# Edge blocks rounded up to 128 records, message stage in 52 table-driven runs

## What is computed

```
# x: (1250, 512); src, dst: (40000,), dst sorted
W   = (softplus(f_ij @ Wf1 + bf1) - log 2) @ Wf2 + bf2   # filter of each edge, 6*128 wide
W   = W * rcut_ij[:, None]                               # (in the model part, per edge)
sj, vj = xs[idx_j], xv[idx_j]                            # gathered by source node, 4*128
s2, v2, w1, t = products of sj, vj with the unit direction u of the edge
x_ij = concat(s2 * W[...], v2 * W[...], w1 * W[...], t * W[...])
agg  = segment_sum(x_ij, idx_i, num_segments=n)          # summed by destination node
```

## Time and profile before

| | us |
|---|---|
| median of three runs | 1356.35 |
| lowest, highest | 1356.25, 1357.49 |
| span of the profiled execution | 1356.8 |
| PE busy | 1237.2 (91%) |
| DVE busy | 1136.8 (84%) |
| POOL busy | 894.8 (66%) |
| ACT busy | 837.5 (62%) |

### The profile page before, as it was taken

One profiled execution on the slowest core, in us unless ns is written; L12 is line 12 of the kernel. 1 busy time (PEld: TensorE's weight loads), 2 busy tenths in 40 slices (PEclk: granted clock), 3 DMA queues, 4 the chain that ended last, 5 costly groups with the idle time before them and its releaser, 6 DMA issues.

```text
span 1356.8 us, 16102 instructions
## 1 busy us (share of the span) xinstructions
PE 1237.2 (91%) x4215; PEld 714.0 (53%) x4215; DVE 1136.8 (84%) x2087; ACT 837.5 (62%) x1851; POOL 894.8 (66%) x796
## 2 busy tenths in 40 slices
PE   5969999999999899899999999999999998977992
PEld 3547777777776563344444444444444433766870
DVE  5888888899999994899999999999999988567325
ACT  3657777777776660766766667666766654774320
POOL 7177777777777675778888888887788832051215
PEclk8979999999999899899999999999999999978995
DMA  9137776878789667888888888888888753644437
GB/s 266 56 131 276 287 272 240 305 292 307 279 300 343 214 238 281 322 305 291 295 298 308 295 294 292 308 303 287 293 304 300 257 169 94 212 169 163 162 118 230
DMA packets 104541, 344.51 MB, mean 254 GB/s; under 512 B 16500, under 2 KB 17436, under 8 KB 94468
## 3 DMA queue, kind: packets, MB, share of 16 engines
q0 software_dynamic: 58496, 192.21, 40.4%
q1 hardware_dynamic: 45956, 151.29, 30.6%
HBM read 216.63 MB, written 126.80 MB: 253 GB/s over the span
## 4 chain that ended last, share of the span: by engine, by line
PE 75%; DVE 7%; issue 5%; POOL 4%; ACT 4%; DMA 3%; SPq 1%; DVEq 0%; POOLq 0%; ACTq 0%
PE PS L2080 21%; PE PS L2085 20%; PE PS L2016 14%; PE PS L2207 6%; PE PS L1894 3%; PE PS L1904 3%; PE PS L1975 2%; PE PS L1983 2%; POOL RR L870 1%; PE PS L2014 1%; PE PS L2187 1%; POOL RR L820 1%; DVE RR L1390 1%; POOL expert_inputs L845 1%; POOL edge_records L783 1%
## 5 line engine op out<-in xcount | busy, mean ns | idle before, releaser
L820 POOL DMA_INDIRECT RR<-node_table,RR x332 | 465.5, 1402 | 143.5 <-issue 90.2
L1065 ACT ACTIVATE RR<-RR 128x256 f32<-128x256 f32 x996 | 407.1, 495 | 230.8 <-PE PS L2085 194.3
L783 POOL DMA_INDIRECT edge_records<-RR x316 | 316.2, 1001 | 112.3 <-issue 67.4
L2080 PE MATMUL PS<-RR 128*125 128x512 f32 x664 | 303.8, 599 | 18.2 <-issue 11.3
L2085 PE MATMUL PS<-RR 128*125 128x512 f32 x664 | 299.3, 592 | 0.0
L2080 PEld LDWEIGHTS PS<-RR 128*125 128x125 f32 x664 | 117.7, 187 | 197.8 <-issue 184.1
L2085 PEld LDWEIGHTS PS<-RR 128*125 128x125 f32 x664 | 124.6, 188 | 160.3 <-issue 160.3
L1390 DVE TENSOR_TENSOR RR<-PS,RR 128x512 f32<-128x512 f32 x237 | 161.4, 686 | 37.7 <-PE PS L2016 35.7
L2016 PE MATMUL PS<-wf_high,h_high 128*128 128x512 f32 x316 | 147.0, 465 | 4.4 <-ACT RR L1019 4.2
L1562 DVE TENSOR_TENSOR RR<-RR 128x1536 f32<-128x1536 f32 (+1 forms) x88 | 146.0, 1659 | 0.0
L2016 PE MATMUL PS<-wf_high,h_low 128*128 128x512 f32 x316 | 126.1, 399 | 0.0
(11 more groups left out here) (346 smaller groups left out, 1855.1 us busy)
## 6 DMA issues: line engine op xcount, KB each, us to landing
RR<-edge_records SPq DMA_DIRECT2D x78, 1040.0 KB, 5.1
expert_inputs<-RR SPq DMA_DIRECT2D x8, 2560.0 KB, 15.3
RR<-in_L_ffn_beta_w SPq DMA_DIRECT2D x8, 1024.0 KB, 7.9
expert_w_raw<-in_L_ffn_expert_w SPq DMA_DIRECT2D x8, 1024.0 KB, 6.8
expert_outputs<-RR SPq DMA_DIRECT2D x27, 256.0 KB, 2.0
edge_records<-RR POOLq DMA_INDIRECT x332, 3.7
RR<-node_table,RR POOLq DMA_INDIRECT x332, 4.3
RR<-edge_records SPq DMA_DIRECT2D x10, 520.0 KB, 3.8
```

What stands on the lines that cost most here:

```text
L783: g.indirect_dma_start(out=rec_dram, out_offset=place, in_=ST[:, j, :], in_offset=None).then_inc(scattered[c], 16)
L820: g.indirect_dma_start(out=GB[:, q % GBS, t, 1:5, :].rearrange("p k n -> p (k n)"), out_offset=None, in_=tab_dram, in_offset=bass.Indirect ...
L1065: last = a.activation(message_slot(q)[:, t, k:k + 5:4, :], GB[:, q % GBS, t, 0:k + 3:k + 2, :], ACT.Copy, scale=record_slot(q)[:, t, 4 * C ...
L2080: te.matmul(PS[0:NT, b, :], OH[:, q % OHS, t, 0:NT], GB[:, q % GBS, t, 1:5, :].rearrange("p k n -> p (k n)"), start=(t == 0), stop=(t == n ...
```

## The change

The blocks are rounded up to 128 records instead of 256, which makes 322 tiles, 10 fewer. The number of filter steps stays 79. `tiles_in(q)` is the number of tiles of a group, `table_entry(run)` the place of a run in the tables. Six empty tiles are left instead of 16, all written ahead of the scatter loop.

The tiles of the message stage are divided into 52 fixed runs of 16, 8, 4, 2 or 1 tiles (`SIZES`; 10, 11, 11, 10 and 10 of them). A run belongs to one block as a whole; which block and which records is worked out on the chip: `run_level(z)` (L1331, 11 small operations of DVE, or 9 for the size of one) gives the runs of one size to the blocks in turn, once for each of five sizes, at steps 8, 14, 20, 26 and 32 of the filter stage; `run_tables` (L1349, 9 operations, two of them 128x550) at step 38 makes the tables `run_sums` (where in the sums) and `run_first_rows` (where in the records). `group_offsets` at step 65, `pair_places` and the second sweep of `places_in_blocks` are gone, and `block_bases` has fewer operations. The wait for the empty places, `places_ready`, moves from the first filter step to the last.

The message stage walks over 81 groups of at most four tiles: runs of 16, 8 and 4 tiles are 4, 2 and 1 groups; 5 mixed groups consist of a two-tile run and two one-tile runs, 2 of two two-tile runs, and 1 of one two-tile run. Large, mixed, middle and four-tile runs alternate. A run has one PSUM bank pair over all its groups, and is flushed once, at the place in DVE's order where the flush of its last group stood: 52 flushes instead of 88. In a mixed group two or three runs end, and as many flushes follow one another. SP loads each piece of a run by a DMA of its own, 93 instead of 88, whose row it reads from the table just ahead.

Core of the diff:

```diff
--- before.py
+++ after.py
+def run_counts(tiles, blocks, sizes):
+
+    left, counts = tiles, []
+    for size in sizes:
+        counts.append((left - blocks * (size - 1)) // size)
+        left -= counts[-1] * size
+    assert left == 0 and min(counts) >= blocks
+    return counts
+
+
+def run_order(sizes, counts):
+
+    large, middle, quad = [[(level, j) for j in range(counts[level])] for level in range(3)]
+    pairs, singles = [[(level, j) for j in range(counts[level])] for level in (3, 4)]
+    mixed = [[pairs.pop(0), singles.pop(0), singles.pop(0)] for _ in range(counts[4] // 2)]
+    mixed += [pairs[k:k + 2] for k in range(0, len(pairs), 2)]
+    assert counts[4] % 2 == 0
+    order = []
+
+    def whole_run(run):
+        order.extend([(run, at, TPQ)] for at in range(0, sizes[run[0]], TPQ))
+
+    while large or middle or quad or mixed:
+        if large:
+            whole_run(large.pop(0))
+        if mixed:
+            order.append([(run, 0, sizes[run[0]]) for run in mixed.pop(0)])
+        if middle:
+            whole_run(middle.pop(0))
+        if quad:
+            whole_run(quad.pop(0))
+    return order
...
-    HALF = GROUP // 2
-    PAIRS = NB
-    QUADS = -(-((E + NB * (HALF - 1)) // HALF - PAIRS) // 2)
-    GROUPS = QUADS + PAIRS
-    NCOL = QUADS * TPQ + PAIRS * TPQ // 2
+    NCOL = (E + NB * (P - 1)) // P
+    SIZES = (16, 8, 4, 2, 1)
+    LEVELS = len(SIZES)
+    RUNS_OF = run_counts(NCOL, NB, SIZES)
+    MAXRUNS = max(RUNS_OF)
+    SCHEDULE = run_order(SIZES, RUNS_OF)
+    RUN = [piece[0] for group in SCHEDULE for piece in group]
+    RUN = [r for n, r in enumerate(RUN) if r not in RUN[:n]]
+    RUNS, GROUPS = len(RUN), len(SCHEDULE)
...
+        def run_of_tile(q):
+
+            return [(RUN.index(run), at + t) for run, at, n in SCHEDULE[q] for t in range(n)]
+
+        def runs_ending(q):
+
+            return [RUN.index(run) for run, at, n in SCHEDULE[q] if at + n == SIZES[run[0]]]
...
-        GOFF_STEP = WO_STEP + 1
-        SPARE_FIRST = 9
-        spare_step = [10 * (n + 1) for n in range(NCOL - LOOPED - SPARE_FIRST)]
-        assert spare_step[-1] < STEPS
+        LEVEL_STEP = [TILE_STEP + PER * (z + 1) - 1 for z in range(LEVELS)]
+        TABLE_STEP = LEVEL_STEP[-1] + PER
...
+            sp.wait_ge(runs_ready, 1)
...
-                rows = quad_rows[q] if q < QUADS else pair_rows[q - QUADS]
-                sp.dma_start(record_slot(q).rearrange("p t r -> p (t r)"), rows)\
-                    .then_inc(rec_in[q % RBS], 16)
+                t0 = 0
+                for run, at, n in SCHEDULE[q]:
+                    c = table_entry(run)
+                    row = sp.value_load(run_row[0:1, c:c + 1], min_val=0, max_val=(NCOL - SIZES[run[0]]) * P)
+                    rows = rec_dram[ds(row + at * P, n * P), :].rearrange("(p t) r -> p (t r)", t=n)
+                    sp.dma_start(record_slot(q)[:, t0:t0 + n].rearrange("p t r -> p (t r)"), rows)\
+                        .then_inc(rec_in[q % RBS], 16)
+                    t0 += n
...
             def places_in_blocks():
 
-                for b in range(NB):
-                    if b:
-                        step(v.scalar_tensor_tensor(srcf, block_mask[b], packed[:, b:b + 1], srcf, ALU.mult, ALU.add))
-                    else:
-                        step(v.tensor_scalar(srcf, block_mask[b], packed[:, b:b + 1], None, ALU.mult))
                 for b in range(NB):
                     step(v.scalar_tensor_tensor(rnk, block_mask[b], off[:, b:b + 1], rnk, ALU.mult, ALU.add))
-
-            def pair_places():
-
-                step(v.tensor_copy(srci, srcf))
-                step(v.tensor_scalar(srci, srci, P.bit_length() - 1, None, ALU.arith_shift_right))
-                step(v.tensor_copy(tB, srci))
-                step(v.scalar_tensor_tensor(srcf, tB, -float(P), srcf, ALU.mult, ALU.add))
-                v.scalar_tensor_tensor(tA, srcf, float(GROUP), rnk, ALU.mult, ALU.is_le)
-                step(v.scalar_tensor_tensor(tB, srcf, -2.0, tB, ALU.mult, ALU.add))
-                step(v.tensor_scalar(tB, tB, float(HALF), float(QUADS * GROUP), ALU.mult, ALU.add))
-                step(v.tensor_tensor(tB, tB, tA, ALU.mult))
-                step(v.tensor_tensor(rnk, rnk, tB, ALU.add))
-
                 v.tensor_copy(posi[:, 0:FULL], rnk[:, 0:FULL])
                 step(v.tensor_copy(posi[0:REM, FULL:RC1], rnk[0:REM, FULL:RC1]))
+
+            def run_level(z):
+
+                cap, size = float(RUNS_OF[z]), float(SIZES[z])
+                if size > 1:
+                    step(v.tensor_scalar(parts, rest, 1.0 / size, -(size - 1.0) / (2.0 * size), ALU.mult, ALU.add))
+                    step(v.tensor_scalar(parts, parts, 1.5 * 2.0 ** 23, None, ALU.add))
+                    step(v.tensor_scalar(parts, parts, -1.5 * 2.0 ** 23, None, ALU.add))
+                else:
+                    step(v.tensor_copy(parts, rest))
+                step(v.tensor_tensor_scan(ends[:, z, :], ones[:, 0:NB], parts, 0.0, ALU.mult, ALU.add))
+                step(v.tensor_tensor(begun, ends[:, z, :], parts, ALU.subtract))
+                v.tensor_scalar(begun, begun, cap, None, ALU.min)
+                step(v.tensor_scalar(ends[:, z, :], ends[:, z, :], cap, None, ALU.min))
+                v.scalar_tensor_tensor(places_of[:, z, 0:NB], begun, -size, cursor, ALU.mult, ALU.add)
+                step(v.tensor_tensor(parts, ends[:, z, :], begun, ALU.subtract))
+                v.scalar_tensor_tensor(cursor, parts, size, cursor, ALU.mult, ALU.add)
+                step(v.scalar_tensor_tensor(rest, parts, -size, rest, ALU.mult, ALU.add))
...
+            def run_tables():
+
+                every = [P, LEVELS, MAXRUNS, NB]
+                v.tensor_tensor(shifts, places_of[:, :, 1:NB + 1], places_of[:, :, 0:NB], ALU.subtract)
+                step(v.tensor_tensor(run_cmp, run_no.unsqueeze(3).to_broadcast(every),
+                                     ends.unsqueeze(2).to_broadcast(every), ALU.is_ge))
+                v.tensor_tensor(run_tile, run_tile, places_of[:, :, 0:1].to_broadcast([P, LEVELS, MAXRUNS]), ALU.add)
+                step(v.reduce_sum(run_no, run_cmp, AX_X))
+                step(v.tensor_tensor(run_cmp, run_cmp, shifts.unsqueeze(2).to_broadcast(every), ALU.mult))
+                step(v.tensor_scalar(goff[:, :], run_no.rearrange("p z j -> p (z j)"), float(NB - 1), float(MSG), ALU.min,
+                                     ALU.mult))
+                step(v.reduce_sum(run_no, run_cmp, AX_X))
+                step(v.tensor_tensor(run_tile, run_tile, run_no, ALU.add))
+                v.tensor_scalar(run_row[:, :], run_tile.rearrange("p z j -> p (z j)"), float(P), None, ALU.mult)\
+                    .then_inc(runs_ready, 1)
...
-                if (i, c) == (0, 0):
+                if i * RING + c == STEPS - 1:
                     dve.wait_ge(places_ready, 1)
...
-            def group_offsets():
-                step(v.tensor_copy(tA[:, 0:GROUPS], goff[:, :]))
-                step(v.tensor_scalar(tB[:, 0:QUADS], tA[:, 0:QUADS], endg[:, 0:1], None, ALU.is_ge))
-                for b in range(1, NB - 1):
-                    step(v.scalar_tensor_tensor(tB[:, 0:QUADS], tA[:, 0:QUADS], endg[:, b:b + 1], tB[:, 0:QUADS],
...
-                elif m == GOFF_STEP:
-                    group_offsets()
+                elif m in LEVEL_STEP:
+                    run_level(LEVEL_STEP.index(m))
+                elif m == TABLE_STEP:
+                    run_tables()
...
-            def flush(q):
-
-                word = dve.value_load(goff[0:1, q:q + 1], min_val=0, max_val=(NB - 1) * MSG)
+            def flush(r, q):
+
+                c = table_entry(RUN[r])
+                word = dve.value_load(goff[0:1, c:c + 1], min_val=0, max_val=(NB - 1) * MSG)
                 dve.wait_ge(summed, tiles(q + 1))
-                if q:
-                    dve.wait_ge(flushed, q)
+                if r:
+                    dve.wait_ge(flushed, r)
                 dst_ap = acc[0:NT, ds(word, MSG)]
-                b = 2 * (q % PSS)
+                b = 2 * (r % PSS)
                 v.tensor_tensor(dst_ap, dst_ap, PS[0:NT, b:b + 2, :].rearrange("p b n -> p (b n)"), ALU.add)\
                     .then_inc(flushed, 1)
...
-                    flush(q - 3)
+                    for r in runs_ending(q - 3):
+                        flush(r, q - 3)
...
             def sums(q):
-                b = 2 * (q % PSS)
-                n = tiles_in(q)
+
+                runs = run_of_tile(q)
                 pe.wait_ge(onehot, tiles(q + 1))
                 pe.wait_ge(d_ready, q + 1)
-                if q >= PSS:
-                    pe.wait_ge(flushed, q - PSS + 1)
-                elif q == PSS - 1:
-                    pe.wait_ge(mix_added, NB)
-                for t in range(n):
-                    te.matmul(PS[0:NT, b, :], OH[:, q % OHS, t, 0:NT],
+                for t, (r, n) in enumerate(runs):
+                    if n == 0 and r >= PSS:
```

(12 more changed lines are left out.)

103 lines of the change are left out of this document (50 added, 53 removed).

## The result

The changed kernel took 1351.71 us (median of 5 runs, 1350.96 to 1353.98) against 1356.35 before, a ratio of 0.9962 with a 95% interval of 0.9945 to 0.9978. It is faster by 4.6 us, where 25 to 26 were forecast; the time lies above the stated range. The profiled execution's span is 1352.2 us.

What follows compares the result with a forecast made beforehand. PE was taken to bound the filter and message stages. -11.4 us up to the first message product and -14.6 in the message stage made -26.0: span 1356.8 to 1330.8, median about 1331, 8-in-10 range 1322 to 1345.

Steps and rivals of the forecast that it cites:

- Startup, -7.0: Ahead of the filter stage: 12.9 us less work on DVE, of which 7.0 us reach PE; bounds 0 and 7.6.
- `group_offsets`, -9.0: Path to POOL's last scatter: dropping its 20 operations and an empty tile saves 9.0 us; bounds 1.3 and 12.5.
- Tables, +4.0: Filter stage: five levels cost 0.3 us each, `run_tables` 2.5, together 4.0 us more; bounds 0 and 10.
- First load, +0.6: First record load on SP: a table register read ahead of it adds 0.6 us; bounds 0 and 2.
- Single flushes, nothing: Message-stage groups with one flush: at most 0.5 us per loop, absorbed by 0.74 us slack of neighbours without flush.
- The mixed groups with three flushes, 19.5: Message stage: five groups at 3.9 us each, 2.9 of waiting and 1.0 for short DMAs and accumulations.
- Rival (a): Message stage: PE's clock falls after the five mixed groups, 3.4 us each, 17 in all, giving 1348; chance 0.12.
- Reserve, 2.0: Message stage: 2 x 1.0 us of waits for what could not be placed.
- The two-tile group, 4.4: Message stage: the group of two tiles costs 4.4 us of waits, its loop through DVE not being proportionally shorter.
- The start, 2.4: Start of the message stage: 2.4 us over the products, the same as in the kernel before.
- (b): Message stage: POOL becomes a moderate second limit, groups at 6.96 to 7.05 us, 1337 to 1341 in all; chance 0.10.
- (d): Message stage: POOL becomes the limit, gathers slowing in 41 groups without flush to 7.96 us per group, 1371; chance 0.03.

Runs made afterwards that it cites:

- before_no_offsets: The kernel before without `group_offsets` at step 65, sums added at other places with otherwise the same work; 1352.15 us, ratio 0.9956 to the kernel before.
- tables_split: The changed kernel with the run tables' 62 operations handed out one to a filter step instead of in bursts; 1348.71 us, ratio 0.9941 to the kernel before.
- per_group: The changed kernel with a flush for every piece of a group (93) instead of one per run (52); 1361.44 us, ratio 1.0036 to the kernel before.
- flush_first: The changed kernel with the flushes ahead of `dot_first` instead of between it and `dot_second`; 1334.86 us, ratio 0.9843 to the kernel before.
- spread: The changed kernel with at most one flush per iteration, later ones queued, still 52 flushes; 1336.06 us, ratio 0.9846 to the kernel before.
- best1: The changed kernel with a four-tile run first, two-tile group last, one flush per iteration, flush ahead of `dot_first`; 1306.36 us, ratio 0.9630 to the kernel before.
- best2: best1 with the run tables' operations also handed out one to a filter step; 1299.88 us, ratio 0.9579 to the kernel before.

## Why the prediction was wrong

The limit (PE), the loop through the two product slots and the terms of the filter stage were right in kind. What failed is the size of three terms of the message stage: single flushes, the two-tile group and the start stood at 6.8 us together and took 31.6. The largest error is the step by which the slack of one group pays for the flush of another.

- **Startup, -7.0:** right, 6.65. Single executions of the later kernels lie up to 2 us on either side.
- **`group_offsets`, -9.0:** right, 9.8 in the path, with `before_no_offsets` behind it.
- **Tables, +4.0:** 6.1. The five levels took 0.65 each instead of 0.3 (I let DVE's mean idle share hide a burst), `run_tables` 2.7 instead of 2.5 (the lead over the kernel before was 4.2 us ahead of it and 1.5 behind). `tables_split` shows that it was the burst.
- **First load, +0.6:** 1.5. No run shows what the register read alone costs.
- **Ten tiles fewer, -17.2:** right; the products take 1.715 us per tile in all these kernels.
- **Single flushes, nothing:** this step failed. I wrote that where groups without flush stand on both sides "their slack of 0.74 takes it". With two slots there is nothing in which slack could be kept: ACT may begin a group when PE has summed the group two before, not earlier, however idle it was. Every loop of 14.25 us pays its 0.53 by itself. 11.0 us in all; `per_group` and `flush_first` show it from both sides. The same holds for the kernel before, where I had worked out the loop and its 0.26 per group, and could have seen that it depends on the flush's place.
- **The mixed groups with three flushes, 19.5:** right in sum, and by luck: 2.9 of wait each, as by the loop, and 5.1 by the clock in three of five cases. The 1.0 us each that I had put for small pieces doesn't show, and the clock stands in its place. Rival (a) had the clock at 3.4 us in all five; it was 1.7 in three.
- **Two flushes, 5.2:** 3.0. **Reserve, 2.0:** not there.
- **The two-tile group, 4.4:** 11.9, the second failed step; 8.8 are waits and 3.1 the clock. The loop through a short group finds 3.43 us less work of PE, and there are two such loops, one through each slot. I priced it from the pair groups in the earlier trace rows, where short groups follow one another and ACT and DVE are short too.
- **The start, 2.4:** 8.65, the third; 2 are the clock. I added 1.0 us for short loads to the interval of each mixed group, and nothing to the start, where no group is loaded ahead yet.
- **The clock, nothing:** the forecast had the gaps of the mixed groups "at a clock of 1.00" and no price for it elsewhere in the stage. It fell behind six gaps and took about 10 us, which are contained in the three items above. Rival (a) put 17 us on it, all behind the mixed groups; half of the 10 stands at the start and around the two-tile group.
- The terms of the message stage: 11.0 + 7.5 + 6.25 - 0.05 - 2.2 - 2.0 + 0.2 = 20.7 us.

Rivals (b) and (d), on POOL, came out wrong; PE's waits go back to gathers at the start only. The Trainium skill's "GPSIMD Engine Reference", Specifications, speaks of contention beside instructions with two SBUF inputs, and I feared for the gathers when the flushes go. No run here shows such a loss: the mean gather took 1402 ns by the page of the kernel before and 1323 after, with 36 flushes fewer. Nor do fewer flushes make it faster: with all 93 of them, in `per_group`, it is 1324, and in `spread`, with 52, 1375. The lines of the pages of the changed kernel and of `per_group` (count, busy us, mean ns, idle before):

```profile
L891 POOL DMA_INDIRECT RR<-node_table,RR x322 | 426.0, 1323 | 182.5 <-ACT RR L1136 81.3
```

```profile
L892 POOL DMA_INDIRECT RR<-node_table,RR x322 | 426.4, 1324 | 189.0 <-issue 88.0
```

## What to carry to other kernels

In a pipeline with two slots, look at each loop by itself: what an operation in it costs is what the loop exceeds the bounding engine's work by, and neither a neighbour's slack nor an idle engine pays for it. So ask first where in the order a short operation stands, then how often it is done: moving it ahead of the operation that waits was worth 18.6 us here, bringing its number from 93 to 52 was worth 9.7. Irregular pieces (a short group, three ends together, three loads for one) each have their own price in such a loop; put them at the end, or hand them out one to an iteration.

## What the hardware showed

Behind a PE gap of 2.6 to 3.6 us in the message stage, the granted clock fell, but not always: in the case shown it was 0.66 over the next 5 us, for 1.7 us of loss. Over nine profiled executions with five groups of three flushes each it happened 27 times in 45, in changing places (all five times in `per_group`, whose gaps were 2.6 to 3.5). Behind the gaps of the groups with two flushes, 18 in the same executions and 1.2 to 1.7 us long, it never did. Behind the gaps of 4.7 us and more, 14 in all runs here, it always did.

In `best1` and `best2`, with no gap over 1.7 us in the stage, the clock did not fall there. That did not end the spread of single executions: the five of `best2` still reach from 1298.9 to 1301.9 us. What makes it is open.
